# Routing and most of the slot filling of a mixture-of-experts layer put inside the turns of the attention before it

## What is computed

```
x = x + xattn0(layernorm(x), ctx)          # 32 heads of 8, axial rotary positions
x = x + ffn0(layernorm(x))                 # only the better half of each sequence's tokens
x = x + xattn1(layernorm(x), ctx)          # 16 heads of 16, heads normalised, 48 main + 16 extra keys
x = x + moe(layernorm(x))
```

```
logits = x @ gate_w.T                      # 64 experts
w, sel = top_k(softmax(logits), 8);  w = w / sum(w)
pos    = position of the token in its expert's list, in token order
valid  = pos < 64                          # 64 slots per expert, the earliest tokens win
y      = sum over a token's valid experts of w * expert(x)     # 256 -> 96 (gate, up) -> 256
```

## Time and profile before

| | |
|---|---|
| median of 3 runs | 1027.32 us (1026.84 to 1027.59) |
| the profiled execution's own time | 1023.76 us |
| its span | 1021.7 us |
| PE busy in the span | 870.0 us (85%) |
| DVE busy in the span | 675.5 us (66%) |
| ACT, POOL busy | 428.3 us (42%), 335.0 us (33%) |
| mean granted TensorE clock | 0.955 of 2.4 GHz |
| DMA moved | 56.61 MB |

### The profile page before, as it was taken

The page is one execution under the profiler, slowest core; times in us unless marked ns, Lnnn a source line. Parts: engine busy times, 40 slices in busy tenths (PEclk is TensorE's granted clock), DMA queues, the critical chain, the costliest instruction groups (busy, mean ns, idle before and its releaser), DMA issues. The chain is left out here.

```text
span 1021.7 us, 25768 instructions
## 1 busy us (share of the span) xinstructions
PE 870.0 (85%) x9240; PEld 667.4 (65%) x9240; DVE 675.5 (66%) x1581; ACT 428.3 (42%) x1027; POOL 335.0 (33%) x293
## 2 busy tenths in 40 slices
PE   0799999999999899999889999999999780088883
PEld 0577777777777688989757777777776660055551
DVE  5577877778777675555367777777776479746552
ACT  1244434444344342233446556655555680023330
POOL 1443433434334040000123333333333010157763
PEclk9899999999999999999989999999999995589997
DMA  9300000000000000000001111111111089965542
GB/s 296 92 13 17 13 13 15 10 15 15 10 15 31 2 8 4 0 0 0 3 11 23 31 31 31 31 28 26 28 31 29 21 293 325 245 172 93 88 74 31
DMA packets 74907, 56.61 MB, mean 55 GB/s; under 512 B 40945, under 2 KB 70001, under 8 KB 74865
## 3 DMA queue, kind: packets, MB, share of 16 engines
q1 hardware_dynamic: 68720, 46.62, 16.2%
q0 software_dynamic: 6144, 9.44, 5.4%
HBM read 41.81 MB, written 14.22 MB: 55 GB/s over the span
## 5 line engine op out<-in xcount | busy, mean ns | idle before, releaser
L404 ACT ACTIVATE pr_t<-bank 128x512 f32<-128x512 f32 x128 | 76.4, 597 | 161.0 <-PE bank L300 160.2
L824 POOL TENSOR_TENSOR g_k_bd<-g_k_t,head_mask 128x1024 f32<-128x1024 f32 x32 | 60.6, 1895 | 134.9 <-ACT g_k_t L999 134.9
L312 PEld LDWEIGHTS bank<-v_bd,pr_t 128*64 128x64 f32 x2048 | 70.0, 137 | 26.5 <-issue 26.3
L300 PE MATMUL bank<-ident,sub 128*128 128x128 f32 x512 | 82.8, 284 | 3.6 <-ACT pr_t L404 2.8
L312 PE MATMUL bank<-v_bd,pr_t 128*64 128x18 f32 x2048 | 82.8, 214 | 0.1
L300 PEld LDWEIGHTS bank<-ident,sub 128*128 128x128 f32 x512 | 56.2, 141 | 31.3 <-issue 17.6
L481 DVE TENSOR_TENSOR sub<-bank,top 128x2048 f32<-128x2048 f32 x32 | 73.3, 2292 | 3.9 <-DVE top L477 0.2
L261 POOL TENSOR_TENSOR rot<-part_a,part_b 128x512 f32<-128x512 f32 x32 | 40.8, 1274 | 103.4 <-DVE part_b L490 103.4
L819 POOL TENSOR_TENSOR xres<-xres,g_out_bias 128x256 f32 (+1 forms) x32 | 23.4, 730 | 153.8 <-DVE g_xn L1022 153.8
L477 DVE TENSOR_REDUCE top<-bank 128x32 f32<-128x2048 f32 x32 | 73.1, 2285 | 0.9 <-PE bank L288 0.8
L648 ACT ACTIVATE f_hid<-bank,b 128x128 f32<-128x128 f32 x128 | 36.6, 368 | 85.5 <-PE bank L594 85.4
(11 more groups left out here) (204 smaller groups left out, 2063.1 us busy)
## 6 DMA issues: line engine op xcount, KB each, us to landing
e_w_gu<-in_experts_in SPq DMA_DIRECT2D x11, 768.0 KB, 10.2
table<-r_row SPq DMA_DIRECT2D x16, 320.0 KB, 9.3
e_w_d<-in_experts_out SPq DMA_DIRECT2D x11, 384.0 KB, 12.1
xres<-in_x SPq DMA_DIRECT2D x4, 1024.0 KB, 9.6
out<-xres SPq DMA_DIRECT2D x32, 128.0 KB, 1.7
xres<-in_experts_in SPq DMA_DIRECT2D x3, 768.0 KB, 21.3
keys_in<-in_ctx_t SPq DMA_DIRECT2D x32, 64.0 KB, 1.8
vals_in<-in_ctx_t SPq DMA_DIRECT2D x32, 64.0 KB, 1.8
```

Source lines behind the costliest of these rows:

```text
L300: m = pe.transpose(b_pr[:, j * P:(j + 1) * P], sub[:, v, cols], k.ident[:, :])
L312: m = pe.matmul(b_o[64 * b:64 * b + 64, hp * VW0:(hp + 1) * VW0], pr_t[:, e, j, b * S:(b + 1) * S], v_bd[:, v, b, hp, :], start=True, stop ...
L404: act.activation(pr_t[:, e, :, :].rearrange("p j q -> p (j q)"), b_pr[:, :], ACT.Exp).then_inc(a_exp, 1)
L824: pool.tensor_tensor(k_bd[:, v, :, :, :, :].rearrange("p c b h s -> p (c b) h s"), k_t[:, v, :, :].rearrange("p c (b a s) -> p (c b) a s", ...
```

## The change

The second attention is not a hardware loop any more but written out, with 39 turns (n = 0 to 38). Pairs of tiles are routed within its turns: the statistics of pair p in turn 2p+6 (even), the picking of experts in turn 2p+7 (odd), the shares and the countdown numbers in turn 2p+8 (even), for 16 pairs. The logits, transposed rows and countdown numbers of the routing share PSUM bank 6 with the value projection, and that projection moves from the first third of PE's turn to its end. Of the slot filling, DVE keeps the 64 largest so far (`best`, CAP = 64) beside each new chunk of 512 columns (four pairs): `work` is 64 + 512 columns wide. Chunks 0 and 1 take one round per turn in turns 16 to 31 (`max` ahead of the residual, `match_replace` ahead of `g_qk`), chunk 2 two rounds per turn in turns 32 to 35, and chunk 3 comes after the last turn. Seven groups of expert weights are loaded in turns 8 to 14, six more after the last tile's residual.

The diff, cut to its core. Sizes, and the turn of PE (`second_attention`, `tensor`), where the value projection (L898 to L909) leaves its place behind L896 and comes back at the end:

```
-RING_E = 9
-OLD_E, MORE_E = 3, 2
-EARLY_E = RING_E + OLD_E + MORE_E
+RING_E, AFTER_E, OLD_E, ROWS_E = 7, 2, 3, 1
+EARLY_E = RING_E + AFTER_E + OLD_E + ROWS_E
...
+PAIRS, ROWS_R, CHUNK = NT // 2, 4, 4
...
                     m.then_inc(g_xnT, 1)
-                if on[2]:
-                    pe.wait_ge(vals_done[u], 32 * i)
-                    if later(a, 1):
-                        pe.wait_ge(g_vc, 2 * a)
...
-                    m.then_inc(g_v, 1)
                 if on[3]:
                     turn(w, v, 1)
...
                     m.then_inc(g_hatT, 1)
+                pe.wait_ge(g_vc, 2 * max(0, min(a, NT)))
+                turned(n)
                 if on[3]:
                     values(w, v, 0)
...
                     m.then_inc(g_out, 1)
+                logits(n)
+                back(n)
                 if on[3]:
                     values(w, v, 1).then_inc(g_pv, 1)
...
                     m.then_inc(g_qkp, 1)
+                if on[2]:
+                    pe.wait_ge(vals_done[u], 32 * i)
+                    pe.wait_ge(k.r_ex, r_marks_read(n))
+                    pe.wait_ge(k.r_found, r_slots_read(n))
...
+                    m.then_inc(g_v, 1)
```

The turn of ACT, where the two copies `g_v_bd` (L1009) move from the end of the turn ahead of the second exponential:

```
                 if on[3]:
+                    act.wait_ge(g_v, w + 1)
+                    if later(w, 2):
+                        act.wait_ge(g_pv, w - 1)
+                    for h in range(2):
...
+                scales(n)
+                if on[3]:
                     exps(1)
...
+                copied(n)
                 if on[1]:
                     act.wait_ge(g_hatT, tk + 1)
...
+                normalise(n)
+                exps_of_route(n)
+                found(n)
```

The turn of DVE: `stats(n)` stands behind `g_xn`, `shifts(n)` behind `g_hat`, `shared(n)` and `fill(n, 0)` behind `g_sub`, `picked(n)` behind the row statistics, `fill(n, 1)` behind `g_halves`:

```
+                stats(n)
                 if on[1]:
                     dve.wait_ge(g_sq_s, tk + 1)
...
+                shifts(n)
                 if on[2]:
...
+                shared(n)
+                fill(n, 0)
                 if on[4]:
                     dve.wait_ge(g_out, f + 1)
...
+                picked(n)
                 if on[3]:
                     dve.wait_ge(g_rcp_s, w + 1)
...
+                fill(n, 1)
                 if on[0]:
                     dve.wait_ge(g_qkp, t + 1)
```

Which pair is at which step in which turn, and the scale of the rows (ACT), which `shifts` on DVE waits for:

```
+def stats_pair(n):
...
+    return (n - 6) // 2 if n % 2 == 0 and 0 <= n - 6 < NT else None
...
+def pick_pair(n):
...
+    return (n - 7) // 2 if n % 2 == 1 and 0 <= n - 7 < NT else None
...
+def slot_pair(n):
...
+    return (n - 8) // 2 if n % 2 == 0 and 0 <= n - 8 < NT else None
...
+        def scales(n):
+            p = stats_pair(n)
+            if p is not None:
+                v = p % 2
+                act.wait_ge(r_moments, 2 * p + 2)
+                act.activation(ln_var[:, v, :], moments[:, v, :, 1], ACT.Ln, bias=k.ln_eps[:, 0:1]).then_inc(r_ln, 1)
+                act.wait_ge(r_ln, p + 1)
+                act.activation(scale[:, v, :], ln_var[:, v, :], ACT.Exp, scale=-0.5).then_inc(r_scale, 1)
...
+        def shifts(n):
+            p = stats_pair(n)
+            if p is not None:
+                v = p % 2
+                dve.wait_ge(r_moments, 2 * p + 2)
+                dve.wait_ge(r_scale, p + 1)
...
+                dve.scalar_tensor_tensor(out=offset[:, v, :], in0=moments[:, v, :, 0], scalar=-1.0, in1=scale[:, v, :],
+                                         op0=ALU.mult, op1=ALU.mult).then_inc(r_offset, 1)
```

The slot filling on DVE:

```
+    rounds, chunks = CAP // 8, PAIRS // CHUNK
+    round_of_turn = {2 * CHUNK * (c + 2) + r: [(c, r)] for c in range(chunks - 2) for r in range(rounds)}
+    round_of_turn.update({NT + t: [(chunks - 2, 2 * t), (chunks - 2, 2 * t + 1)] for t in range(rounds // 2)})
...
+        def largest(c, r):
+            area = work[:, 0 if c else CAP:CAP + CHUNK * P]
+            if r == 0:
+                dve.wait_ge(k.r_found, CHUNK * (c + 1))
...
+                dve.tensor_copy(work[:, CAP:CAP + CHUNK * P], k.fresh[:, :]).then_inc(s_taken, 1)
+                if c:
+                    dve.tensor_copy(work[:, 0:CAP], best[:, :]).then_inc(s_kept, 1)
...
+            dve.max(best[:, 8 * r:8 * r + 8], area).then_inc(s_max, 1)
...
+        def without(c, r):
+            area = work[:, 0 if c else CAP:CAP + CHUNK * P]
             if r < rounds - 1:
...
+                dve.match_replace(area, best[:, 8 * r:8 * r + 8], area, 0.0).then_inc(s_rep, 1)
...
+        def fill(n, half):
+            todo = round_of_turn.get(n, [])
+            if len(todo) == 2:
+                largest(*todo[half])
+                without(*todo[half])
+            elif todo:
+                (largest, without)[half](*todo[0])
```

The queue of SP in the second attention and behind it (`program`, `sync`):

```
+            for t in range(NT):
+                g_both(t, t // 2, t % 2)
+                if t >= 6:
+                    g_store(t - 6)
+                if t >= 8 and t % 2 == 0:
+                    r_store((t - 8) // 2)
+                if t == 8:
+                    sp.wait_ge(k.f_x2, NT)
+                if 8 <= t < 8 + RING_E:
+                    load_experts(sp, ins, k, t - 8)
+            r_store(PAIRS - 4)
+            r_store(PAIRS - 3)
+            for t in range(NT - 6, NT):
+                g_store(t)
+            sp.wait_ge(k.g_raw_s, NT)
+            for n in range(RING_E, RING_E + AFTER_E):
+                load_experts(sp, ins, k, n)
+            r_store(PAIRS - 2)
+            r_store(PAIRS - 1)
...
```

More of the change, by code:

```diff
@@ L784, in store, with gpsimd @@
                 sp.wait_ge(g_x3, t + 1)
[L785 to L796, removed]
+                sp.dma_start(k.out[t * P:(t + 1) * P, :], k.xres[:, t, :]).then_inc(k.out_set, 16)
+            return both, store
+        def gpsimd(pool, weigh):
             pool.wait_ge(k.a_x1, NT)
@@ L946, in step, with scalar @@
                     m.then_inc(g_qkp, 1)
+                if on[2]:
+                    pe.wait_ge(vals_done[u], 32 * i)
+                    pe.wait_ge(k.r_ex, r_marks_read(n))
+                    pe.wait_ge(k.r_found, r_slots_read(n))
+                    if later(a, 1):
+                        pe.wait_ge(g_vc, 2 * a)
+                    else:
+                        pe.wait_ge(k.f_pickTc, NQ)
+                    for kind in range(2):
+                        for b in range(2):
+                            for h in range(2):
+                                m = pe.matmul(b_v[64 * h:64 * h + 64, kind * D + b * P:kind * D + (b + 1) * P],
+                                              vals_in[:, u, kind, b * S:(b + 1) * S], k.wv1[:, kind, h, :], start=True, stop=True)
+                    m.then_inc(g_v, 1)
             return step
-        def scalar(act):
+        def scalar(act, scales, copied, normalise, exps_of_route, found):
             act.wait_ge(g_fill, 4 + 8)
@@ L984, in step @@
                 if on[3]:
+                    act.wait_ge(g_v, w + 1)
+                    if later(w, 2):
+                        act.wait_ge(g_pv, w - 1)
+                    for h in range(2):
+                        rows = slice(64 * h, 64 * h + 64)
+                        act.activation(v_bd[rows, v, :, :, 0:4 * HD1].rearrange("p b n (e f d) -> p f e (b n) d", e=2, f=2)[:, h],
+                                       b_v[rows, :].rearrange("p (e m d) -> p e m d", e=2, d=HD1), ACT.Copy).then_inc(g_vc, 1)
+                scales(n)
+                if on[3]:
                     exps(1)
@@ L1279, in fill_slots @@
      s_name_s, s_token, s_move
-     ) = z.sems(
-         "s_max s_rep s_turn s_turnc s_back s_backc s_max2 s_rep2 s_dup s_last s_value_s s_empty_s s_name_s "
+     ) = own.sems(
+         "s_taken s_kept s_max s_rep s_turn s_turnc s_back s_backc s_max2 s_rep2 s_dup s_last s_value_s s_empty_s s_name_s "
          "s_token s_move")
-    rounds = CAP // 8
-    def first_of(dve, found, best, max_done, rep_done):
-        for r in range(rounds):
-            if r:
-                dve.wait_ge(rep_done, r)
-            dve.max(best[:, 8 * r:8 * r + 8], found).then_inc(max_done, 1)
-            if r < rounds - 1:
-                dve.wait_ge(max_done, r + 1)
-                dve.match_replace(found, best[:, 8 * r:8 * r + 8], found, 0.0).then_inc(rep_done, 1)
@@ L1673, in _ @@
             f.gpsimd(pool)
-            g_step = g.gpsimd(pool)
-            turns(pool, g_step, NT, 5)
-            for n in range(NT, NT + 4):
+            g_step = g.gpsimd(pool, r.gpsimd(pool))
+            for n in range(last_turn + 1):
                 turn(g_step, NT, 5, n)
-            r.gpsimd(pool)
         @block.tensor
@@ L1704, in _ @@
             turn(f_step, NQ, 4, NQ + 2)
-            turns(pe, g_step, NT, 5, 2)
-            turn(g_step, NT, 5, NT)
-            turn(g_step, NT, 5, NT + 1)
-            r_step = r.tensor(pe)
-            r_step(0)
-            turn(g_step, NT, 5, NT + 2)
-            r_step(1)
-            turn(g_step, NT, 5, NT + 3)
-            for n in range(2, routing):
-                r_step(n)
+            for n in range(2, last_turn + 1):
+                turn(g_step, NT, 5, n)
             s.tensor(pe)
```

507 lines of the change are left out of this document (246 added, 261 removed).

## The result

The changed kernel takes 1046.83 us (median of 4 runs, 1046.0 to 1050.65), the kernel before 1027.09 beside it: ratio 1.0199, interval 1.0173 to 1.0225. It is slower by 20 us, where 6 us less was forecast. The profiled executions differ by 22.3 us of span (1044.0 against 1021.7).

A forecast was written before the change was run, and what follows sets the result against it. PE was taken to bound the second attention's turns (8.88 us). Turns 38.4 us longer and a tail of 47.1 end the first filling 7.9 earlier; SP's queue adds 2: -5.9 from 1027.32 gives 1021.4 us (1004 to 1036).

The forecast's parts named there:

- SP's queue: In turns 8 to 14, keys issued behind weights and table come late: 2 us taken, bounds 0 and 7 x 2.
- Value projection moved: At the end of PE's turn it makes each turn 9.35 us, 0.45 more, bounds 0 and 1.0.
- Turns 1 to 7: Early turns of the second attention: turns 2 to 5 cost 1.8 us more, turns 6 and 7 cost 2.1.
- Logits: Routing in PE, odd turns: four logits matmuls for a pair take 0.43 us.
- The wait of DVE for the scale: Even turns with routing: the shift holds DVE until ACT has the scale, 0.9 us.
- Turns 16 to 31: Turns with filling, bound by DVE: even 10.35 us, odd 10.65, 25.9 us more in all.
- Copies: Two copies more, a chunk 0 of 512 columns and no replace in the last rounds: together -0.8 us.
- Tail: From the end of turn 32's `g_hat` to the end of the first filling: 47.1 us, ending at 870.9.
- From there to the experts: Stretch from the end of the first filling to the experts' first matmul stays at 10.7 us.
- A: Rival: turns bound by sums of work, 9.5 us each, 1000 us; sign: two-turn period below 19.5; chance 0.13.
- B: Rival: TensorE clock falls inside the turns, 1036 us; sign: clock below 0.98 in 560 to 800; chance 0.17.
- C: Rival: keys late by the upper bound, or written-out code costs 0.2 us a turn; 8 to 10 us more; chance 0.15.

The follow-up runs named there:

- run 2: Kernel before with only the value projection moved to the end of PE's turn, its two copies ahead of the second exponential: 1046.6 us, ratio 1.0218.
- run 4: Changed kernel with the next tile's keys issued right behind this tile's values, ahead of stores, table and weights: 1035.84 us, ratio 1.0098.
- run 6: Changed kernel with the seven groups of expert weights of turns 8 to 14 loaded behind the last residual: 1041.82 us, ratio 1.0183.
- run 1: Kernel before with the four loops of the second attention written out: ratio 0.9975.
- run 3: Changed kernel with the value projection back between scores and heads, its copies back at the end of ACT's turn: 1018.45 us, ratio 0.9931.
- run 9: Changed kernel with DVE's copies into the work area written as a reduction over one element: 1044.5 us, ratio 1.0201.
- run 10: The kernel of run 7 with each round's eight largest written straight into the other work area, so no copies are left: 1010.64 us, ratio 0.9857.
- run 7: Changed kernel with three edits: value projection back in its place, keys ahead of weights, two work areas: 1013.87 us, ratio 0.9913.
- run 5: Changed kernel with ACT writing transposed values straight into one of two work areas, without DVE's copies of 128x512: 1042.65 us, ratio 1.0184.
- run 8: Changed kernel with DVE's copies into the work area written as a maximum of the source with itself: 1050.34 us, ratio 1.0269.

## Why the prediction was wrong

The forecast was -5.9 us and the span grew by 22.3: 28.2 us to account for. By stretches of the profiled execution they are 0.65 (`g_hat` 1 later), 1.7 (turns 1 to 7), 11.6 (8 to 15), 3.1 (16 to 31), 1.1 (a slip, below), 6.8 (tail) and 3.1 (experts). The step that failed most is the price of SP's queue, 2 us for 10; then the tail, 47.1 for 53.9, and the moved value projection, 0.45 us a turn for 0.65. Step by step:

- **Value projection moved (+0.45 a turn, bounds 0 and 1.0).** Right in kind, mis-sized: 0.65 measured (run 2), each half of the turn being 0.1 us short. Together with what hangs on it, undoing it gave back 27 us, where this term and the queue's stood for 15.5.
- **SP's queue (2 us, bounds 0 and 14).** The largest error. I saw that the sum "just fails to fit" and priced the near end. Measured: 10 us (runs 4 and 6), nearly all in turns 8 to 15, which took 94.2 us where my turns and this term give 82.5. The bound held; the choice did not. It also lacked a term: behind the longest wait (2.19 us) the clock was down for the next instructions, so the price was the wait and more. Turn 13 paid 3.4 us (14.65 against 11.2) for one late load of 64 KB.
- **Turns 1 to 7.** 5.6 us more than before where 3.9 stood in the sum, and `g_hat` 1 starts 0.65 late. Turn 2 took 11.64 us, with the clock at 0.93 in its window; with the projection back it took 8.02. Turns 1 and 2 together scatter, 17.8 us in run 1 and 20.9 in the kernel before, whose work is the same.
- **Logits (0.43 us a pair).** 1.00: a pair is half of the 16 matmuls of a group, not a quarter, a slip of the working. It counts in full where PE binds: turn 7 took 11.21 us against 9.53 for turn 5 without routing, 1.68 more where 1.1 was forecast. In turns 8 to 15 that is 2.3 us. The wait of DVE for the scale was 0.57 and not 0.9.
- **Turns 16 to 31 (21.0 a pair).** 21.0 measured, by luck and for another reason: I had them bound by DVE, but they are bound by PE's chain with the late projection. Only run 3 showed DVE's bound, 20.5. A number that comes out right does not show its reason.
- **Copies (-0.8 with other small terms).** A copy cost 1.6 and 1.8 us of turns 16 and 24 (11.41 and 11.64 against 9.81), all that turns 16 to 31 took above the forecast. I priced it as if POOL did not work beside it; the copy of 0.67 us in its place (run 9) leaves 0.3 and 0.6.
- **Tail (47.1).** 53.9. The copy of chunk 2 took 2.16 us beside `g_k_bd` (846.15). DVE waited 2.57 us for the scale of turn 34's pair, where 0.9 stood, because PE's value projection, and ACT's work behind it, had waited 2.99 us for `r_ex` (the exponentials of the routing), which came behind two rounds of filling on DVE. The profile calls both waits "issue"; `r_ex` is what ends last ahead of the projection (859.30), by the program's order. The last pair's chain, from the scale to the copy, took 8.0 us (876.82 to 884.79) where 5.9 stood, with the logits at the lower clock (1.97 us for 1.00). These make up most of the 6.8 us; the rest I did not divide.
- **From there to the experts (10.7)** was right. **The experts** took 3.1 us more. DVE's first copy of `e_part` waits 4.08 us for something that the profile calls remote, which before waited 1.97 for PE; it begins 15.3 us into the stage in place of 13.3, and PE's eight matmuls behind it (L1533) take 2.79 us for 1.99 at the lower clock. That is 2.8 of the 3.1. Run 3 waits 4.21 us there, put down to PE at the lower clock, and its experts take 134.0 us; run 10 waits 4.09 for the remote thing again and takes 135.6 (before 132.2). What is waited for stays open.
- The last 1.1 us are mine: `g_hat` of turn 32 came 9.98 us behind that of turn 31 in the kernel before, not 8.88.

**The rivals.** A (sums of work, 9.5 us a turn) is out: the turns took 9.81 and 11.20 us. B (the clock falls in every turn) is out as put: the windows from 650 to 850 keep 1.00 with PE waiting 0.7 us each turn. The Trainium skill (TensorE: Matmul & The Clock Gate, section HAM oscillation) tells of a loop whose waits for DMA between groups of matmuls bring the clock down each time. Those waits are longer than the 0.7 us here, so that section does not make B the forecast for these turns, as the prediction had it, and the windows show no such fall. In the falls within turns 8 to 31 that I looked at, the clock went down behind a wait of 2.19 us (turn 13), one of 1.82 (run 7), and in run 5 behind three of 0.65 us and less; in run 8 a wait of 1.82 us for keys (625.53) was followed by none. So the length of the last wait alone does not tell it, and what else counts stays open. C was the mechanism in its first half, and its price was too small: the keys at 10 us, within their upper bound, and the clock with them. Of the prediction's signs of being wrong only C's came, PE's seven waits for DMAs. With the projection left in place the change's idea does pay, if by little: ratio 0.9931, and 0.9825 with the waits taken out that the runs found.

## What to carry to other kernels

An instruction that fills a hole in the bound engine's turn costs nothing where it stands and its whole length elsewhere: price a move by the hole it leaves, and look at what its end releases, here the next loads in SP's queue. Where the working says that a transfer just fails to arrive, take the far bound and allow for a fall of the clock behind the wait. Small loads that a turn needs belong ahead of large ones that nobody waits for yet, and a DVE copy beside a long POOL instruction costs the rest of that instruction, however short the copy is.

## What the runs showed of the hardware

- DVE beside a POOL TENSOR_TENSOR that began first: a COPY of 128x64 ended 0.05 us, a COPY of 128x512 0.28 us and a TENSOR_TENSOR of 128x512 with both inputs in SBUF 0.55 us behind POOL's end. That held beside 1.89 us of POOL (rows of 1.75, 1.98 and 2.25 us) and beside 0.40 us (0.44, 0.67 and 0.93). A TENSOR_REDUCE of 128x512 took 0.67 to 0.69 us beside either.
- After a single wait of PE of 1.82 us (run 7) and 2.19 us (after) the next instructions ran at the lower clock (1.43 and 1.98 us for 1.09); after another of 1.82 us (run 8) and after waits of 0.7 us in every turn they did not, and in turn 25 of run 5 they did behind waits of 0.65, 0.39 and 0.51 us.
- With 319 GB/s of loads under way, the wait at the change of stage was 7.00 us where it was 2.03 in the changed kernel, and that for the first gather 9.51 where it was 4.90.
